# Moving weight casts and the first norm's affine terms between ScalarE, VectorE and GpSimd in an attention and mixture-of-experts kernel

## The reference, cut to what matters

```python
def _L0_xattn_ref(h, adj_raw, Wq, Wk, gamma_raw):          # h is the context, adj_raw is layernorm(x)
    ...
    sim = jnp.einsum('bhnd,bhmd->bnm', Q, K) / (jnp.sqrt(jnp.float32(d)) * H)
    k = max(1, int(n * TOP_K_RATIO))                        # 76 of 256
    topk_vals = jax.lax.top_k(sim, k)[0]
    threshold = topk_vals[:, :, -1:]
    sparse_mask = (sim >= threshold).astype(sim.dtype)
    A_learned = jax.nn.sigmoid(sim) * sparse_mask
    A_learned = (A_learned + jnp.swapaxes(A_learned, -1, -2)) * 0.5
    gamma = jax.nn.sigmoid(gamma_raw)
    return (1.0 - gamma) * adj_raw + gamma * A_learned
...
x = x + _L0_xattn_ref(ctx_512, _layernorm(x), Wq, Wk, gamma_raw)
x = x + _L0_ffn_ref(_layernorm(x), gate_w, fc1_w, fc1_b, fc2_w, fc2_b, alpha)   # gelu experts, top 2 of 8
```

## Time and profile before

| what | value |
| --- | --- |
| median of 3 runs | 130.39 us (130.18 to 130.52) |
| the profiled execution | 130.1 us, its span 128.3 us |
| TensorE matmul busy | 119.2 us (93%) |
| VectorE busy | 96.2 us (75%) |
| ScalarE busy | 87.6 us (68%) |
| GpSimd busy | 65.0 us (51%) |
| granted TensorE clock | 1.000 over the whole span |

### The profile page before, as it was taken

One profiled execution on the slowest core, in us unless ns is written; L12 is line 12 of the kernel. 1 busy time (PEld: TensorE's weight loads), 2 busy tenths in 40 slices (PEclk: granted clock), 3 DMA queues, 4 the chain that ended last, 5 costly groups with the idle time before them and its releaser, 6 DMA issues.

```text
span 128.3 us, 2763 instructions
## 1 busy us (share of the span) xinstructions
PE 119.2 (93%) x904; PEld 108.6 (85%) x904; DVE 96.2 (75%) x399; ACT 87.6 (68%) x212; POOL 65.0 (51%) x66
## 2 busy tenths in 40 slices
PE   6796989899969999999999999999999999999990
PEld 3443656699949999999899999998999999999990
DVE  0068989886987898999979999999787337823481
ACT  3178999899999979454897784729646544555510
POOL 2039668638647944643097456512972545444400
PEclk9999999999999999999999999999999999999999
DMA  2999999952996000002000000200000002000002
GB/s 66 198 390 415 405 321 174 192 101 29 181 169 119 5 0 3 0 5 82 3 0 0 3 8 0 81 1 8 0 0 0 5 0 82 0 5 0 3 0 82
DMA packets 3380, 10.05 MB, mean 78 GB/s; under 512 B 396, under 2 KB 868, under 8 KB 3364
## 3 DMA queue, kind: packets, MB, share of 16 engines
q1 hardware_dynamic: 2500, 6.71, 14.7%
q0 software_dynamic: 864, 3.15, 14.3%
HBM read 8.81 MB, written 1.05 MB: 77 GB/s over the span
## 4 chain that ended last, share of the span: by engine, by line
PE 41%; DVE 36%; ACT 13%; issue 6%; POOL 1%; DVEq 0%; POOLq 0%; ACTq 0%
PE p_y L477 17%; PE p_h L455 16%; DVE acc L1061 8%; ACT h_act L579 3%; ACT w_lo L564 2%; ACT w_hi L557 2%; DVE top L886 2%; DVE above L842 2%; DVE stats L745 2%; ACT h_hi L587 2%; PE p_y L355 2%; DVE left L891 1%; DVE picked L1018 1%; ACT act_waste L543 1%; DVE best_f L1004 1%
## 5 line engine op out<-in xcount | busy, mean ns | idle before, releaser
L698 POOL TENSOR_TENSOR h_lo<-h_act,h_hi 128x512 fp32r<-128x512 f32 x31 | 40.2, 1300 | 45.4 <-ACT h_hi L587 32.6
L579 ACT ACTIVATE h_act<-p_h,small_sb 128x256 f32<-128x256 f32 x64 | 26.6, 467 | 19.4 <-PE p_h L455 19.3
L455 PE MATMUL p_h<-xt_hi,w_hi 128*128 128x256 f32 x128 | 32.9, 280 | 1.1 <-ACT h_act L579 1.0
L455 PE MATMUL p_h<-xt_hi,w_lo 128*128 128x256 f32 x128 | 32.6, 278 | 0.0
L1061 DVE SCALAR_TENSOR_TENSOR acc<-p_y,comb,acc 128x256 f32<-128x256 f32 x55 | 24.0, 475 | 11.0 <-PE p_y L477 10.2
L477 PE MATMUL p_y<-w_hi,h_hi 128*128 128x256 f32 x126 | 26.0, 288 | 1.0 <-DVE acc L1061 1.0
L455 PEld LDWEIGHTS p_h<-xt_hi,w_hi 128*128 128x128 f32 x128 | 24.1, 188 | 1.6 <-issue 1.5
L455 PE MATMUL p_h<-xt_lo,w_hi 128*128 128x256 f32 x128 | 25.3, 279 | 0.0
L477 PE MATMUL p_y<-w_lo,h_hi 128*128 128x256 f32 x126 | 24.9, 279 | 0.0
L477 PE MATMUL p_y<-w_hi,h_lo 128*128 128x256 f32 x126 | 24.9, 279 | 0.0
L455 PEld LDWEIGHTS p_h<-xt_hi,w_lo 128*128 128x128 f32 x128 | 24.1, 188 | 0.0
(11 more groups left out here) (141 smaller groups left out, 191.1 us busy)
## 6 DMA issues: line engine op xcount, KB each, us to landing
w_sb<-w SPq DMA_DIRECT2D x8, 512.0 KB, 8.3
w_lo<-w POOLq DMA_DIRECT2D x6, 512.0 KB, 5.6
x_sb<-x SPq DMA_DIRECT2D x1, 768.0 KB, 8.5
out<-acc SPq DMA_DIRECT2D x3, 256.0 KB, 2.5
x_sb<-x SPq DMA_DIRECT2D x1, 256.0 KB, 4.4
out<-acc SPq DMA_DIRECT2D x2, 128.0 KB, 2.0
attn_sb<-attn SPq DMA_DIRECT2D x1, 192.0 KB, 5.1
small_sb<-small SPq DMA_DIRECT2D x1, 97.5 KB, 4.7
```

Of the source, the lines that this page charges most:

```text
L455: last = nc.tensor.matmul(dst, w_[:, e, 0, k, c * P:(c + 1) * P], v[:, b % 2, k, :], start=n == 0, stop=n == len(trio) - 1)
L579: last = nc.scalar.activation(h_act[:, s % 2, c], tiled(p_h[s % 2])[:, c, :], ACT.Gelu, bias=b1_sb[:, e, c:c + 1])
L698: nc.gpsimd.tensor_tensor(h_lo[:, s % (LAG + 1)], h_act[:, s % 2], h_hi[:, s % (LAG + 1)], ALU.subtract).then_inc(h_lo_ready, 1)
```

## The change

High parts: GpSimd now makes those of experts 0, 1, 2, 5, 6 and 7, ScalarE those of 3 and 4. ScalarE's negated parts of experts 4 to 7 are in steps 0, 1, 1 and 3, its `base(1)` in step 3 instead of step 2, and its cast of `b2` in step 5. GpSimd issues `weight_rest(3)` later and `weight_rest(4)` to `weight_rest(7)` in steps 0 to 3. The affine terms of batch 0 and `base(0)` stand directly behind `weight_lo(0, 0)` on GpSimd, ahead of the casts of experts 1 and 2. Gamma's terms are made at the start, from small operands that are loaded second.

```diff
-POOL_HI = 3
+POOL_HI = (0, 1, 2, 5, 6, 7)
+ACT_HI = (3, 4)
+POOL_HI_AT = {0: 6, 2: 7}
@@ SyncE
             sp.dma_start(attn_sb[:, 0:first], attn[:, 0:first]).then_inc(attn_in, 16)
+            sp.dma_start(small_sb[:], small).then_inc(small_in, 16)
             sp.dma_start(x_sb[:, 0], x[:, 0:TILES]).then_inc(x_in[0], 16)
             sp.dma_start(attn_sb[:, first:], attn[:, first:]).then_inc(ctx_in, 16)
-            sp.dma_start(small_sb[:], small).then_inc(small_in, 16)
@@ ScalarE
             u_copy(0)
+            act.wait_ge(small_in, 16)
+            nc.scalar.activation(gam[:, 0:1], gamma_sb, ACT.Tanh, scale=0.5).then_inc(gam_th, 1)
+            nc.scalar.activation(gate_parts[:, :, 0], gate_sb, ACT.Copy).then_inc(gate_hi_ready, 1)
             sim_copy(0)
...
             sigmoid(0)
+            weight_hi(3)
+            sim_copy(1)
+            spread_of(1)
             weight_neg(2)
-            weight_hi(3)
             weight_neg(3)
...
-            weight_hi(5)
+            weight_hi(4)
...
-                if s < 3:
-                    weight_neg(5 + s)
                 if s < 2:
-                    weight_hi(6 + s)
-                if s == 3:
+                    weight_neg(4 + s)
+                if s in (1, 3):
+                    weight_neg(6 + s // 2)
+                if s == 5:
                     act.wait_ge(b2_in, 16)
...
                     sigmoid(b + 1)
-                    base(b + 1)
+                    if b:
+                        base(b + 1)
+                if s == 3:
+                    base(1)
@@ GpSimd
+            def ln1_affine(b):
+                pool.wait_ge(gam_ready, 1)
+                pool.wait_ge(ln1_agg, (b + 1) * TILES)
+                pool.wait_ge(ln1_rstd, b + 1)
+                for t in range(TILES):
+                    nc.gpsimd.tensor_scalar(mul1[:, b, t:t + 1], rstd1[:, b, t:t + 1], gam[:, 2:3], ones[:], ALU.mult,
+                                            ALU.add)
+                    last = nc.gpsimd.tensor_scalar(add1[:, b, t:t + 1], mv1[:, b, t, 0:1], gam[:, 3:4],
+                                                   rstd1[:, b, t:t + 1], ALU.mult, ALU.mult)
+                last.then_inc(ln1_mul, 1)
@@ VectorE
             nc.vector.memset(warm[:], 1.0).then_inc(warm_set, 1)
+            gamma_terms()
...
             flag_few(0)
-            gamma_terms()
             drop_above(0)
-            ln1_affine(0)
             take_eight(0)
...
-                if s == 4:
+                if s == 6:
                     b2_parts_of()
```

More of the change, by code:

```diff
@@ L559, in weight_neg @@
             def weight_neg(e):
-                if e < POOL_HI:
-                    act.wait_ge(w_hi_early, e + 1)
+                if e in POOL_HI:
+                    act.wait_ge(w_hi_early, POOL_HI.index(e) + 1)
                 else:
-                    act.wait_ge(w_hi_ready, e - POOL_HI + 1)
+                    act.wait_ge(w_hi_ready, ACT_HI.index(e) + 1)
                 nc.scalar.activation(w_lo[:, e], w_hi[:, e], ACT.Copy, scale=-1.0).then_inc(w_neg_ready, 1)
@@ L608, in _ @@
             signs_again_of(0)
-            act.wait_ge(small_in, 16)
-            nc.scalar.activation(gam[:, 0:1], gamma_sb, ACT.Tanh, scale=0.5).then_inc(gam_th, 1)
             for b in range(1, BATCHES):
@@ L613, in _ @@
             sigmoid(0)
+            weight_hi(3)
+            sim_copy(1)
+            spread_of(1)
             weight_neg(2)
-            weight_hi(3)
             weight_neg(3)
-            for b in range(1, BATCHES):
+            for b in range(2, BATCHES):
                 sim_copy(b)
-            nc.scalar.activation(gate_parts[:, :, 0], gate_sb, ACT.Copy).then_inc(gate_hi_ready, 1)
-            spread_of(1)
-            weight_hi(4)
-            weight_neg(4)
             signs_of(1)
@@ L708, in _ @@
             weight_lo(0, 0)
-            weight_hi(1)
-            weight_hi(2)
+            ln1_affine(0)
             base(0)
-            weight_lo(1, 0)
-            weight_rest(2)
             pool.wait_ge(gate_hi_ready, 1)
@@ L716, in _ @@
                 gate_lo_ready, 1)
-            weight_rest(3)
-            pool.wait_ge(masked, TILES)
-            weight_lo(0, 1)
-            rstd(veps2, rstd2, 0, ln2_veps, ln2_rstd)
-            weight_rest(4)
-            pool.wait_ge(xn_ready, TILES)
+            weight_hi(1)
+            weight_hi(2)
+            weight_lo(1, 0)
+            weight_rest(2)
+            rstd(veps2, rstd2, 0, ln2_veps, ln2_rstd)
+            pool.wait_ge(xn_ready, TILES)
+            weight_lo(0, 1)
+            weight_rest(3)
             weight_lo(1, 1)
+            weight_hi(5)
             for s in range(STEPS):
@@ L728, in _ @@
                     hidden_lo(s)
-                if s == 0:
+                if s == 1:
                     rstd(veps1, rstd1, 1, ln1_veps, ln1_rstd)
-                if s < 3:
-                    weight_rest(5 + s)
+                if s < 4:
+                    weight_rest(4 + s)
+                if s in POOL_HI_AT:
+                    weight_hi(POOL_HI_AT[s])
                 if more and b and e == 0:
```

## The result

The changed kernel takes 136.70 us in the median of 4 runs (136.49 to 137.08), against 130.37 for the kernel before (130.18 to 130.52). The ratio is 1.049, with a 95% interval of 1.046 to 1.052: slower by 6.3 us. The forecast was 130.1, in a range of 129.3 to 130.8, with 0.16 for slower. It was wrong.

A forecast was written before the change was run, and what follows sets the result against it. VectorE was taken to bound the start of the steps, ScalarE `up(5)`, TensorE the late stretch. The 0.22 us opening gain lies within `up(5)`'s 0.28 us, limited by expert 5's DMA: median 130.39 to 130.1, range 129.3 to 130.8.

The forecast's parts named there:

- The bound of before: TensorE full from 94.00 to 122.60; the start of the steps bound by VectorE, `up(5)` by ScalarE.
- the part on the steps: ScalarE's relief moves `gelu(3)` to about 34.4; expert 5's DMA then sets `up(5)` at 38.32, 0.28 us earlier.
- The wait for VectorE before `down(2)`: TensorE's wait of 0.44 us at 36.02, claimed to go because ScalarE gives the tanh a cast earlier.
- the rule: VectorE instructions with two SBUF inputs contend with GpSimd ones reading SBUF; the second to issue fully blocks.
- The second rival: GpSimd's queue from `xn` to `weight_rest(5)` stretches by four collisions at 0.31, 1.2 us; median 131.3; chance 0.16.
- decision point: In the steps: `weight_rest(5)` issued later than 33.4 instead of the forecast 32.72 would favour the second rival.
- a blocked `choose`: In the opening, `choose` waits for `weight_lo(1, 0)`, ending at 17.06 instead of 16.37; 0.69 us given back.
- The opening: Ahead of the steps: VectorE has 0.91 us less, 0.69 given back, so everything from the mask on is 0.22 earlier.
- the loads: In the opening, same bytes in another order ahead of the first expert's weights, so no delay: nothing taken.
- A: GpSimd's time for the four affine terms in the opening, taken as 1.0 us, 0.25 each; bounds 0 and 2.2.
- The weights' DMAs: In the steps, `weight_rest(4)` lands at 34.50, its wait inside the next; `weight_rest(5)` at 38.32, releasing `up(5)`.
- The wait of `up(5)` for ScalarE: TensorE's wait of 0.96 us before 38.60, claimed to go as `gelu(3)` moves from 37.65 to about 34.4.

The follow-up runs named there:

- fill_read: The kernel before, with one more GpSimd copy of 128x1024 to a spare tile behind each weight DMA of steps 0 to 2: 136.73 us, ratio 1.0489.
- casts_earlier: The changed kernel, with GpSimd's casts of experts 5 and 6 moved into its wait ahead of the second norm's rstd: 130.18 us, ratio 0.9983.
- picks_in_psum: The changed kernel, with the second pick and the sum `weight` in spare PSUM columns, GpSimd's list untouched: 131.92 us, ratio 1.0099.
- third_lo_later: Changed kernel's opening, `weight_lo(1, 0)` moved behind `xn`, GpSimd waiting for `add_masked` after its casts, on the steps of `casts_in_gap`: 130.10 us, ratio 0.9972.
- casts_in_gap: The kernel before, with the casts of experts 5 and 6 moved from ScalarE into GpSimd's wait ahead of step 0: 129.49 us, ratio 0.9917.
- opening_only: The changed kernel's opening on the steps of the kernel before: runs of 130.85, 133.43, 133.74 and 134.23 us, no ratio.
- gamma_first: `casts_in_gap` with gamma's terms first, small operands loaded second and the gate's high part early: 131.73 us, ratio 1.0089.
- affine_clear: `gamma_first` with affine terms on GpSimd, and expert 2's cast and what follows behind `add_masked`: runs of 132.41 to 132.97 and 134.98 to 135.28 us, ratio 1.0185.

## Why the prediction was wrong

**The bound of before** was read rightly: the late stretch is full in both kernels, and 6.2 of the 6.4 us stand ahead of `up(6)`.

**The step that failed** is this sentence of the part on the steps: "The wait for VectorE before `down(2)` goes too, as ScalarE gives the gap's tanh a cast earlier." It became 4.39 us. The tanh was not late: it stands at 30.96 in after and at 30.97 in before. But VectorE, which read it at 31.27 before, comes to it at 33.65, held by `best_f`, and then stands 3.09 in `weight`. The prediction looked at who feeds VectorE and not at what VectorE's own picks meet on GpSimd. It had the rule and two rows for it, and used it for the opening alone. In the steps it noted that GpSimd would have no gap from `xn` to step 3, and priced that as a queue for the weights' DMAs. `fill_read` shows that this gap was what VectorE lived on: three copies that nobody waits for make 6.3 us. `casts_earlier` gives the gap back to the changed kernel, and the loss is gone. `picks_in_psum` shows it from the other side.

**The second rival** (0.16) had the right sign and the right port, but the wrong victim and size: "four collisions at 0.31" on GpSimd's side, 131.3. Its decision point, `weight_rest(5)` issued later than 33.4, was just not reached (33.38), and the loss was there. What starved was VectorE. One of its rows for GpSimd waiting is weaker than it looks: the record of the `weight_lo` of 1.58 starts before the DMA issue ahead of it ends, at 19.32 + 0.88 = 20.20, and from there it takes 1.31.

**A wait priced by one instruction.** Even where the prediction expected a blocked `choose`, it let it end with the first GpSimd instruction. Had the same been done in the steps, `weight` would have cost up to the end of one cast, 1.8 us, against 3.09 measured.

**The opening**: -0.22 forecast, +0.64 measured. VectorE's 0.91 us less is right: in `third_lo_later` the first `chosen` stands at 16.25, 0.81 earlier than in the earlier trace rows. That `choose` is blocked is right. Its end at 17.06 is wrong by 1.0: the loads, taken as nothing, delay GpSimd's first cast from 8.47 to 9.17, 0.70 in this pair of profiles; and A, taken as 1.0, is 1.39 (four rows of 0.33 to 0.34, with their spacing). Both terms stood in a list with no slack. The estimate of 1.2 from the Trainium skill, GPSIMD Engine Reference, its opening and section 3.1 (GpSimd about twice as slow as VectorE), was nearer; the row is 1.39 beside VectorE's 0.61, so here it is 2.3 times as slow in operations of one column.

**The weights' DMAs**: `up(4)` waits 0.92 for its one, which the prediction had inside the next wait; in `picks_in_psum`, where it isn't hidden, it is 0.56. The wait of `up(5)` for ScalarE went, as forecast: `gelu(3)` starts at 35.72 instead of 37.65. That its row shows no wait proves little in after, where `down(2)` ahead of it is 5.8 late, but in `picks_in_psum` it has none either. With `casts_in_gap` the same relief of ScalarE is worth 0.9 us.

**The clock** was not a term of the sum. Behind long waits of TensorE it came on top: 1.4 us in after; in the profiled run of `opening_only`, 3.77 above the median before, 1.37 are left beyond `xn`'s 2.40; in `gamma_first` 0.80. The last two are remainders and may hold more than the clock.

**What stays open**: at which ends of GpSimd's instructions a waiting VectorE instruction gets in, and why. In after, `left` at 27.40 gets in behind a cast that ends at 28.45, with the next instruction recorded at 28.52; `best_f` doesn't get in behind the cast that ends at 31.78, with the next one recorded at 31.45. But `left` in `third_lo_later` gets in behind the `h_lo` that ends at 29.39, though an `rstd` is recorded at 29.02. A gap in the records was enough, and not always needed. Where it was not, the next record is each time the two-column `rstd`: `best_f` in after gets in at 33.04 beside one recorded from 32.71, and `left` in `affine_clear` behind an `h_lo` that ends at 31.50 beside one from 31.16; before's `best_f` takes 0.17 beside one. That so small an instruction doesn't block would fit all four, but no run tests it. The starts of the records don't tell who came first either: the cast behind the DMA issue of 35.76 is recorded from 36.35, 0.6 into the issue, and `weight`, recorded from 35.96, waited for it all the same.

## What to carry to other kernels

A wait of GpSimd can be what lets VectorE work: before filling GpSimd's gaps, list VectorE's instructions with two SBUF inputs, and its copies, casts and tensor_scalars from SBUF to SBUF, that stand beside them, and put GpSimd's work where VectorE has none on its path (130.18 us here, against 136.70 with the same casts a few places further on). Small tiles that VectorE passes to itself can go to PSUM, which took 4.8 us off here. In an opening, a wait of GpSimd that looks idle (1.24 us for the gate's part) can be the slot in which `add_masked` runs, so an operand that is ready earlier can make a kernel slower.

## What the runs showed of the hardware

- A VectorE instruction of 128x8 waited 6.16 us through two reading and two writing GpSimd instructions and the DMA issues between them, and 6.43 with copies; one of 16 columns waited 3.09. So the wait isn't bounded by the end of the first GpSimd instruction.
- With two SBUF inputs, VectorE passed a memset (`chosen` 0.22 beside it, as alone) and a DMA issue behind which GpSimd waited (`add_masked` 0.75 beside it, as alone).
- One-column tensor_scalars with two pointer scalars take 0.33 each on GpSimd, one behind the other.
- With the load of 97.5 KB moved ahead of two others, the first cast of the weights behind them started at 8.71 to 9.55 in eight profiles, against 7.86 to 8.47 in six, at the same bytes.
- After TensorE waited 2.63, 3.16 and 4.39 us, the granted clock was 0.58, 0.56 and 0.74 in the stretches behind (`gamma_first` 24 to 27, `opening_only` 24 to 30, after 43 to 48); after waits of 0.4 to 1.3 it stayed at 1.00. Between these the last wait alone doesn't tell: after 1.62 in `affine_clear` it was 0.72 from 24 to 30, after 1.63 in `picks_in_psum` 1.00 from 20 to 24.
